# Attention stage on Trainium2: normalised x for the projections from a second, transposed copy of x, made on GpSimd, in place of TensorE transposes

## What is computed

```python
m = mean(x); v = var(x); xn = (x - m) / sqrt(v + eps)
Q, K, V = xn @ W_q.T, xn @ W_k.T, xn @ W_v.T        # 16 heads of 32
for each segment of 64 rows:
    sq, sk = elu(q) + 1, elu(k) + 1
    A_mem = (sq @ M) / (sum(sq * z) + EPS)
    A_dot = softmax(causal(q @ k.T * scale)) @ v
    A_s   = beta * A_mem + (1 - beta) * A_dot
    M    += sk.T @ (v - (sk @ M) / (sum(sk * z) + EPS))
    z    += sum(sk)
out = A @ W_o.T
```

## Time and profile before

| | |
|---|---|
| median of 3 runs | 1945.66 us (1945.05 to 1948.57) |
| profiled execution, its own time | 1945.36 us |
| its span, first to last instruction | 1943.6 us |
| mean granted TensorE clock | 0.985 |
| TensorE busy | 1848.5 us (95%) |
| VectorE busy | 1445.2 us (74%) |
| ScalarE busy | 875.7 us (45%) |
| GpSimd busy | 148.7 us (8%) |
| DMA | 108.45 MB, mean 56 GB/s |

### The profile page before, as it was taken

How to read it: one execution, slowest core, us unless ns; L and a number is a source line. 1 busy time by engine, 2 the same in 40 slices (tenths; PEclk the granted TensorE clock), 3 DMA queues, 4 the chain that set the end, 5 groups by cost and what they waited for, 6 DMA issues and landing times. The chain is left out here.

```text
span 1943.6 us, 72290 instructions
## 1 busy us (share of the span) xinstructions
PE 1848.5 (95%) x32348; PEld 1567.1 (81%) x32348; DVE 1445.2 (74%) x3477; ACT 875.7 (45%) x1494; POOL 148.7 (8%) x179
## 2 busy tenths in 40 slices
PE   6999999999999999999999999879899999879998
PEld 5888888888888888888888888657677777667997
DVE  6888788888887777787777777667588788876222
ACT  4443334343434443444434343325588787764110
POOL 2000000000000000000000000041100000001000
PEclk9999999999999999999999999879999999999999
DMA  4111211121121112111111110236500000015000
GB/s 147 47 46 58 73 52 46 58 74 52 46 74 52 36 36 61 43 36 40 59 41 36 47 51 30 95 95 183 164 26 12 13 12 23 13 41 161 17 12 22
DMA packets 65139, 108.45 MB, mean 56 GB/s; under 512 B 4720, under 2 KB 25216, under 8 KB 64832
## 3 DMA queue, kind: packets, MB, share of 16 engines
q1 hardware_dynamic: 59056, 84.69, 14.0%
q0 software_dynamic: 5776, 19.15, 3.2%
HBM read 59.26 MB, written 27.26 MB: 45 GB/s over the span
## 5 line engine op out<-in xcount | busy, mean ns | idle before, releaser
L1083 PE MATMUL proj<-xnT_high,held 128*128 128x256 f32 x1536 | 235.2, 288 | 3.3 <-DVE xnT_low L782 2.4
L1083 PEld LDWEIGHTS proj<-xnT_high,held 128*128 128x128 f32 x1536 | 203.6, 191 | 9.2 <-DVE xnT_low L782 2.9
L444 POOL TENSOR_TENSOR xs<-xs 128x512 f32<-128x512 f32 x63 | 80.9, 1285 | 1170.0 <-DVE xs L885 1170.0
L1083 PE MATMUL proj<-xnT_low,held 128*128 128x256 f32 x1024 | 163.7, 281 | 0.0
L2088 DVE CUSTOM_DVE_ANT_0 Sm<-Sp,held 128x1023 f32<-128x1023 f32 x128 | 155.5, 1216 | 8.0 <-DVE xs L2076 2.0
L1986 ACT ACTIVATE Sm<-Sm,least 128x1023 f32<-128x1023 f32 x128 | 146.7, 1146 | 14.1 <-DVE least L2088 13.3
L1083 PEld LDWEIGHTS proj<-xnT_low,held 128*128 128x128 f32 x1024 | 140.1, 190 | 0.0
L2141 PE MATMUL Sp<-KS,held 128*128 128x512 f32 x256 | 94.4, 451 | 29.9 <-DVE least L2088 25.6
L506 ACT ACTIVATE Pq<-Pq 128x1024 f32<-128x1024 f32 x63 | 66.9, 1062 | 123.4 <-DVE Pq L848 123.3
L486 ACT ACTIVATE QT<-proj 128x512 f32<-128x512 f32 x64 | 38.1, 595 | 182.4 <-PE proj L1083 182.4
L2038 DVE COPY PTs<-Tp 128x512 f32<-128x512 f32 x128 | 88.3, 690 | 29.7 <-PE Tp L2153 29.2
(11 more groups left out here) (343 smaller groups left out, 4341.2 us busy)
## 6 DMA issues: line engine op xcount, KB each, us to landing
VS<-DV SPq DMA_DIRECT2D x64, 264.0 KB, 3.9
xs<-in_x SPq DMA_DIRECT2D x32, 512.0 KB, 4.8
out_rows<-xs SPq DMA_DIRECT2D x64, 256.0 KB, 2.0
mask_columns<-x1T SPq DMA_DIRECT2D x16, 512.0 KB, 5.2
xs<-in_w SPq DMA_DIRECT2D x16, 512.0 KB, 3.8
xe<-in_x SPq DMA_DIRECT2D x15, 512.0 KB, 3.5
QT<-in_wqT SPq DMA_DIRECT2D x1, 1024.0 KB, 6.5
KT<-in_wkT SPq DMA_DIRECT2D x1, 1024.0 KB, 9.4
```

The lines of the kernel that those rows point to most:

```text
L444: pool.tensor_tensor(Ass[k], T1s[k], T2s[k], ALU.add).then_inc(s_as, 1)
L1083: ins = pe.matmul(bank[:, g * BT:g * BT + BT], w[hw][:, c, o:o + P], xnT[hx][:, c, :], start=n + c == 0, stop=n == 2 and c == G - 1)
```

## The change

x also comes in as `xT`, turned on the host (512 rows of 8192). From block 2 on, TensorE no longer turns xn. In its place, in pass m for block m + 2: SP loads the turned x (512 KB) into the space of the former second xn buffer (`turned`); SP stores the block's means and factors 1/sqrt from `mv` and `rstd` to DRAM (`row_stats`) and reads them back broadcast over all partitions (`MR`, 256 KB); GpSimd subtracts the means and multiplies by the factors in four operations of 128 x 512 (`turned_rows`), between its two additions; ScalarE makes xnT_high in one copy (`high_x`), VectorE xnT_low in one subtraction (`low_turned`). `normalise` still writes xn rows for the blocks whose router score is computed from them (block number below 17). The lists ORDER, and the order of the calls in `half` of TensorE, VectorE and ScalarE, are new.

```diff
+            def row_factors(m):
+                sp.wait_ge(s_mv, m + 1)
+                if m > 0:
+                    sp.wait_ge(s_mrr, 16 * m)
+                sp.dma_start(row_stats[0:1, :].rearrange("o (a p) -> p (o a)", p=P), mv[:, 0:TILES, 0],
+                             allow_slow_non_contiguous=True).then_inc(s_mrw, 16)
...
+                sp.wait_ge(s_mrw, 32 * (m + 1))
...
+                sp.dma_start(MR[:, :, :].rearrange("p w t -> p (w t)"),
+                             row_stats.rearrange("w t -> (w t)").rearrange("(o n) -> o n", o=1)
+                             .broadcast_to([P, 2 * BT])).then_inc(s_mrr, 16)
...
+            def turned_rows(m):
+                pool.wait_ge(s_xT, 16 * (m + 1))
+                pool.wait_ge(s_mrr, 16 * (m + 1))
+                for k in range(2):
+                    c = slice(2 * k, 2 * k + 2)
+                    pool.tensor_tensor(turned[:, c, :], turned[:, c, :], bm(MR[:, 0, :], 2), ALU.subtract).then_inc(s_xn, 1)
...
             def half(m):
-                for a in range(TILES):
-                    rows(m * 2 + a, m, a)
+                rows(m * 2, m, 0)
+                if m + 2 < NB:
+                    turned_rows(m)
+                rows(m * 2 + 1, m, 1)
...
+            def high_x(m):
+                act.wait_ge(s_xn, 4 * m + 4)
+                got(act, "V1", m)
+                copy(xnT[0][:, :, :], turned).then_inc(s_th, 1)
...
+            def low_turned(m):
+                dve.wait_ge(s_th, m + 1)
+                dve.tensor_tensor(xnT[1][:, :, :], turned, xnT[0][:, :, :].bitcast(F32),
+                                  ALU.subtract).then_inc(s_tl, 1)
...
-        ORDER = (["AST1", "OUT1", "KT0", "KT1", "V1", "SK1", "DEN", "OUT0"],
-                 ["QT0", "QT1", "AST0", "V0", "SK0", "XT0", "XT1"])
+        ORDER = (["AST1", "OUT1", "KT0", "AST0", "V0", "SK0", "DEN"],
+                 ["QT0", "QT1", "KT1", "V1", "OUT0", "SK1"])
```

More of the change, by code:

```diff
@@ L258, in order @@
                 skip = ("AST1", "OUT1")
-            if m == NB - 2:
-                skip = ("XT0", "XT1")
             if m >= NB - 1:
-                return [["OUT1"], ["AST1"]][b] if m == NB else [u for u in ORDER[b] if u in STAGE2]
+                return [["OUT1"], ["AST1"]][b] if m == NB else [["AST1", "OUT1", "AST0", "OUT0"], []][b]
             return [u for u in ORDER[b] if u not in skip]
-        STAGE2 = ("AST0", "OUT0", "AST1", "OUT1")
         def offers(n):
@@ L341, in half @@
                     store(m - 1, m * 2 - 2, 0, "OUT0")
+                if ln:
+                    if first:
+                        sp.wait_ge(s_mv, 1)
+                    else:
+                        sp.wait_ge(s_tl, m)
+                    sp.dma_start(turned, xT_t[m + 2]).then_inc(s_xT, 16)
+                if not first:
                     store(m, m * 2 - 1, 1, "OUT1")
+                if ln:
+                    row_factors(m)
                 if m == NB - 2:
@@ L900, in last @@
                 pn = 1 - p
+                denominators(m - 1, m * 2, p)
+                reciprocals(p)
                 previous_values(m - 1, p)
@@ L932, in half @@
                 if not first:
-                    out_rows(m - 1, m * 2 - 2, pn, 0)
+                    low_a(m, m * 2 - 1, 1)
+                    denominators(m - 1, m * 2, p)
+                    reciprocals(p)
                 previous_values(None if m == 0 else m - 1, p)
-                if not first:
-                    low_a(m, m * 2 - 1, 1)
                 if stage1:
@@ L940, in half @@
                     ahead_moments(m)
+                if ln:
+                    statistics(i + 1, p, m)
                 if choice:
@@ L944, in half @@
                     out_rows(m, m * 2 - 1, pn, 1)
+                softmax_part(m, 0)
                 m_next(m, 0)
-                softmax_part(m, 0)
+                if ln:
+                    deviation(2 * TILES if look else TILES)
+                    if not first:
+                        dve.sem_inc(s_mv, 1)
                 if first:
-                    router(p, wcol[:, 0:2])
+                    router(0, wcol[:, 0:2])
                 if m + 1 < AHEAD:
-                    router(pn, wcol[:, (m + 1) * 2:(m + 1) * 2 + 2])
+                    router(m + 1, wcol[:, (m + 1) * 2:(m + 1) * 2 + 2])
+                if first:
+                    dve.sem_inc(s_mv, 1)
                 if choice:
@@ L982, in half @@
                 memory_part(m, p, 1)
-                if ln:
-                    low_x(m, (m + 2) * 2, "XT", 0)
-                m_next(m, 3)
                 if look:
                     ahead_router(m, 1)
-                if stage1:
-                    denominators(m, n2, pn)
-                    reciprocals(pn)
                 if ln:
-                    low_x(m, (m + 2) * 2, "XT", 1)
+                    low_turned(m)
+                out_rows(m, m * 2, p, 0)
+                m_next(m, 3)
             def beta_factors():
@@ L1069, in feature @@
                         moved(pe, f"{before[0]}{x}", before[1])
+                tokens = 0 if m is None else m + 1
+                if tokens > 1 and name == "QT" and k == 0:
+                    pe.wait_ge(s_th, tokens - 1)
                 bank, full = take(pe, f"{name}{k}", m)
@@ L1081, in feature @@
                             moved(pe, "XF1", None)
+                        if tokens > 1 and name == "QT" and k == 0 and g == 0 and hx:
+                            pe.wait_ge(s_tl, tokens - 1)
                         for c in range(G):
@@ L1287, in half @@
                     out_proj(m, 1)
+                a_and_b(m, p, 0)
+                pv(m, mh, p, 0)
                 t_times_m(m, 0)
[L1289 removed]
                 if stage1:
@@ L1324, in half @@
                         scores(pn, 1)
-                if ln:
-                    x_transposes(m, m + 2, p, "XT", 1)
-                out_proj(m, 0)
+                    den_transposes(m)
+                    sk_rows(m, n2, 1)
             pe.wait_ge(s_const, 1)
```

85 lines of the change are left out of this document (48 added, 37 removed).

## The result

The changed kernel takes 2119.72 us, median of 4 runs (2117.28 to 2123.43). The kernel before, measured beside it, takes 1947.12 us (4 runs, 1945.05 to 1951.57). The ratio is 1.0885, with a 95% interval of 1.0859 to 1.0911: 172.6 us slower. The forecast was 1942.6, the range 1927 to 1962.

What follows compares the result with a forecast made beforehand. TensorE's full queue was taken as the bound. Passes 15 to 29 gain 6.8 us, passes 0 to 14 lose 3.0, first and last lose 1.0: 2.8 off 1945.36 gives 1942.6 us, range 1927 to 1962.

Steps and rivals of the forecast that it cites:

- What I cost at nothing, and its cover: Transfers, GpSimd's four operations, xnT copies and moved VectorE pieces: all hidden under other work, priced at nothing.
- Rival 4: Row chain: both transfers over 12 us make xnT_high late in all passes, each us over costing 30 us; chance 0.05.
- What goes away: TensorE's queue: 60 groups of four transposes, XT0 and XT1 in 30 passes, leave; 0.9 us a pass, 27 us gained.
- First new wait: TensorE at QT0 waits for ScalarE's SK1 copy to free PSUM bank 1; 0.45 us in 30 passes, 13.5 us.
- Second new wait: TensorE's second P transposes wait for the exponential, as GpSimd's addition slows VectorE's residual; 0.65 us in 15 passes.
- the prediction's first rival: One of the two waits, for QT0's bank or VectorE's port, is missing: 1929 or 1933 us; chance 0.22.
- Rival 3: GpSimd's four operations hold VectorE up after the second softmax in passes 0 to 14; 1955 to 1975 us, chance 0.23.
- the rival's worse case: GpSimd's operations block VectorE for two full blocks after the second softmax, in 15 passes: 32 us lost, 1975 us.

Runs made afterwards that it cites:

- the 16 B kernel: The changed kernel with means and factors packed by VectorE into one store of 128 pieces of 16 B a pass; 1965.74 us, ratio 1.009.
- early rows: The changed kernel with its two stores made in pass 0 only, later passes using the rows of block 2; 2008.01 us, ratio 1.0306.
- The gate: The changed kernel with stores in pass 0 only and GpSimd's four operations held behind the second softmax; 1957.1 us, ratio 1.0069.
- the last version: The 16 B kernel with SK1 ahead of the den_transposes, residual on ScalarE, and ahead_rows on ScalarE in passes 0 to 14; 1957.8 us, ratio 1.0042.

## Why the prediction was wrong, point by point

**The step that failed** is the paragraph "What I cost at nothing, and its cover". It priced the row chain by the nearest rows, broadcasts of 2.7 and 5.1 us, and asked only whether the rows arrive in time. The chain from the first store to the landed rows took 13 to 16 us (8.4 to 11.1, and 4.6 for the read) in place of 5.4 to 10.2. Rival 4 had the place right ("a 4-byte element per packet has no row here, so this stays open"). But it decided from 12 us of lateness and had a chance of 0.05, and the mechanism is another one. TensorE did not wait for late rows: its list has no large wait for xnT_high. GpSimd alone waited for them (272.4 us, 60 to 1220 us), off the critical path. With stores that nobody waits for the loss is 123.5 us all the same. A store in flight was taken for a thing that costs only those who wait for it.

**What the stores do.** Shown: pieces of 4 B side by side in DRAM, from different partitions, land only after 8.4 to 11 us. In the second half of that time TensorE stops with "issue" in 24 of 30 passes, and its clock falls behind the gap. VectorE stops with "remote" for over 1 us in 11 passes and ScalarE in 7 (60 to 1400 us). These 18 stops all stand at an instruction that waits for a semaphore of TensorE, and by the trace's semaphore records that signal comes 0.02 to 0.03 us before they end. So it isn't shown that these two engines are held themselves: TensorE's late signals would look the same, and VectorE starts less_max inside 8 of TensorE's 23 such gaps over 1.5 us. GpSimd is held too: with the two stores added to the kernel before, its addition starts 4.2 us after its last signal in 5 passes, those where the signal comes within 1 us ahead of a store's issue, and in 3 passes with the 128 neighbouring pieces. In the kernel before, with pieces apart, or with pieces of 16 B or 512 B this never happens.

Shown too: it takes both, the size and the neighbourhood. 4 B pieces apart cost nothing at either number, and 128 pieces of 16 B side by side, in the 16 B kernel, land in 2.0 us (median). The number goes with how much is lost (65 us for 128 a pass, 123.5 for 512). A trace holds one thing more, the queue that loads instructions. From before, the page's row of that queue (packets, MB, share of 16 engines' span), which makes 0.009 x 16 x 1943.6 / 256 = 1.09 us a packet:

```profile
q8 instruction: 256, 4.19, 0.9%
```

After, the answer on DMA for 592 to 593.3 us, just ahead of the gap above, with one packet:

```profile
DMA packets 1, 0.02 MB, mean 13 GB/s; under 512 B 0, under 2 KB 0, under 8 KB 0
...
q8 instruction: 1, 0.02, 18.3%
```

18.3% of 16 x 1.3 us is 3.8 us. By the records of single packets it begins at 592.76 and ends at 596.57, and TensorE goes on at 596.95. Between 60 us and the stage's end, packets of this queue over 2 us number 1 before and 1 or 2 with 4 B pieces apart, 30 in the changed kernel, 32 with its stores added to the kernel before, and 40 with 128 pieces side by side. In the changed kernel 29 of the 30 begin 1.2 to 11.4 us behind a store's issue. So loads of instructions are often slowed while such a store is in flight. That the engines stop for want of instructions fits the pass above, but not all rows: only 7 of TensorE's 40 gaps over 1 us (60 to 1400 us) end within 1.2 us of the end of such a slow packet. In the passes whose stores are issued at 147, 191, 235, 324 and 413 us TensorE stops for 1.2 to 2.8 us at a time, beginning 5.0 to 6.3 us behind the store, while no packet of the queue takes over 1.93 us. At 501 and 854 us there are packets of 3.42 and 3.18 us and no such gap. Why the engines stop stays open; slow loads of instructions may be a companion and not the cause. The Trainium skill ("DMA: Bandwidth & Descriptors", Specifications) says that below 512 B a DMA engine reads, modifies and writes. No run here shows that step. Pieces of 4 and of 16 B, 32 B apart, are below 512 B too and cost nothing here, so by these runs small size alone is not enough. What inside the chip collides wasn't tried.

**"What goes away"**: right that the groups go. The price of 0.9 us a pass, 27 in all, can't be seen in the changed kernel. In the 16 B kernel TensorE's busy time falls by 14.8 us over the span, and by 17.9 us from 60 us to the last matmul of out_proj. So this term was put too high by 9 to 12 us; that the other slots stay as they are was an assumption. Part of it may be the clock (mean 0.983 against 0.985); which part isn't shown.

**First new wait**: right in place and number, and a little too dear. It was put at 0.45 us, 30 times, 13.5 us; it is 0.34, 29 times, 9.9 us. The timeline at the end of a pass:

```profile
573.70 0.66 PE L1171 MATMUL proj<-ident,SKT 128*128 128x128 f32 x4 [0.93 <-DVE xs L953]
574.19 0.60 PE L1309 MATMUL proj<-ident,xs 128*128 128x128 f32 x4
575.13 1.18 PE L1151 MATMUL proj<-xnT_high,held 128*128 128x256 f32 x8 [0.34 <-ACT SK L514]
```

**Second new wait**: the mechanism is right. Residual takes 2.02 us beside GpSimd's addition (591.03 above; 2.05 forecast). In the changed kernel the wait is rare, since the stalls come first. In the 16 B kernel it is there 10 times, 0.65 us on average (6.5 us), where 15 times 0.65 was forecast: the size is right, the number too high.

**What I left without a price**: SK1, at 573.70 above, waits behind den_transposes for VectorE's out_rows, 10 times, 7.5 us. The prediction gave VectorE 0.1 to 0.4 us of slack at the den_transposes just ahead, did not look at SK1's own wait for the bank, and took both for nothing. VectorE came later: in each of the first 15 passes low_turned starts 0.67 us behind GpSimd's second addition and takes 2.06 us (the addition 1.65). In the other 15 it starts 0.16 us ahead of it and takes 1.22 us, and the addition takes 2.2. So whichever starts first makes the other wait, as the prediction's first rival said of the port.

```profile
570.98 2.06 DVE L844 TENSOR_TENSOR xnT_low<-xs,xnT_high 128x1024 fp32r<-128x1024 f32 x1
```

GpSimd's own durations were taken as 1.29 us: its addition now takes 1.58 (page, above), its subtraction 1.33, and in the 16 B kernel, where it reads with a step of four, 1.59 and 1.84 for subtraction and product.

**Rival 3**, that GpSimd's operations hold VectorE up (1955 to 1975), names the time of the kernel once the stores are harmless (1965.74 us with late rows), but the mechanism in part only. Of the 33.5 us that TensorE is idle more there, 10.2 and 6.5 are the forecast's own two waits, 4.5 are SK1's, which fits the rival, and the rest is spread over small ones. With early rows it reaches 2008.01, past the rival's worse case, because the four operations then fall before the second softmax, not behind it. I had given it 0.23 and the forecast 0.45. The gate shows that it is their place that counts, but only for early rows. With the 16 B store and no other relief, holding them back moved VectorE's delay to SK1. The Trainium skill ("SBUF — State Buffer", Who interferes with whom) expects a lock for the whole instruction where VectorE has two SBUF inputs or uses a two-port mode beside a GpSimd instruction that reads SBUF. The trace agrees: residual 2.02 us in place of 1.01, low_turned 2.06 in place of 1.22, and the longer GpSimd rows.

**Still open**: why the last version, with no named wait of weight left, is 1.0042 and not under 1. It has 20 us more of gaps than the kernel before (36.2 against 16.0), and TensorE's busy time is 9.3 us less (1839.2 against 1848.5), not the 27 us of the forecast. Why the removed groups give back only a third of their price isn't shown.

## What to carry to other kernels

A small store that spreads one number per partition over neighbouring words of DRAM is not free because nobody waits for it: here 30 pairs of them cost 123.5 us. Write rows of 512 B, pieces of 16 B, or pieces 32 B apart; in these runs all of them cost nothing or next to it. And when a queue is full and its neighbours have slack of tenths of a microsecond, price the second-order waits one by one: the transposes taken out of TensorE's order came back as waits of 0.3 to 1.8 us each on different partners, and most edits that removed one made another longer.

## What the runs showed of the hardware

- 128 pieces of 4 B: side by side in DRAM, one store a pass adds 65 us over 30 passes; 32 B apart, it lands in 1.4 us and adds nothing (0.9982). 512 pieces of 4 B apart land in 2.5 us and add nothing (1.0001).
- TensorE's stall begins about 5 us behind the issue, not at once. In 26 of the 30 passes the pieces' own packets are over within 3 us of it, and the store still counts as landed only after 8.4 us or more.
- "issue" on TensorE inside a group of equal matmuls (L1244, 22 times, 53.1 us), with a DMA share of 0.00 in the pass shown, was the mark of it, often with "remote" on ScalarE or VectorE; packets of the instruction queue went from 1.1 us to as much as 3.9.
- After a gap of some 4 us TensorE ran at the 1.2 GHz level: groups of four at 1.05 to 1.20 us in place of 0.63 to 0.74. A mean clock of 0.94 over 997 us of work makes an estimate of 60 us in the changed kernel, which is enough for the 48.7 us by which its busy time grew.
- GpSimd is slowed too where it slows VectorE: its addition, on operands of the same shape, went from 1.285 us to 1.585 us on average.
- low_turned (128x1024, both inputs in SBUF) takes 2.06 us where GpSimd's addition started 0.67 us before it and 1.22 us where it started 0.16 us before the addition; the addition then takes 2.2 us, against 1.65 (15 passes each).
